# T5 attentions of a vision tower: scores per image on the rows of two heads, probabilities divided before they are turned, outputs made in turned form

## The chip, the cores and the metric

One core of a Trainium2 chip runs the whole tower in one launch. The metric is the device time in microseconds; shown are three runs of the kernel before and one profiled execution. TensorE's granted clock stands at one of two levels, 2.4 GHz (1.0 in the profile) or 1.2 GHz (0.5).

## The reference, cut to what matters

32 images of 37 tokens (a class token and 36 patches), width 192, 12 heads everywhere. The tower makes tokens, then three attentions with heads of 16 (neighbour, causal with a capacity MoE behind it, diagonal-masked), then four T5 layers, each an attention with heads of 64 and a feed-forward; the second and fourth of these have a routed MoE beside the dense one. Only the four T5 attentions compute something differently here:

```
q, k, v = nx @ attn_q[i], nx @ attn_k[i], nx @ attn_v[i]     # (b, 37, 12 heads, 64)
scores  = einsum('bqhd,bkhd->bhqk', q, k) + bias             # bias[h, q, k], the same for all images
attn    = softmax(scores, axis=-1)
ctx     = einsum('bhqk,bkhd->bqhd', attn, v).reshape(b, s, 768)
h       = h + ctx @ attn_o[i]
```

All in float32. There is no scale on the scores and no mask: each image attends to its own 37 tokens.

## The kernel before, in words

**Tiling.** Three images make a group of TG = 111 rows, 11 groups in all. Groups are taken in blocks of 3, 3, 3 and 2 for the q and k projections. A T5 attention has, per block, 12 QK steps (six chunks of q, then six of k; a chunk is 128 of the 768 columns, two heads, turned, so that tokens lie along the free axis), and per group two V steps (six heads each), two S steps, PT, PV, OT steps and a Y step.

**Order.** One list, PROGRAM, gives the order of the steps (`att_order`, line 351, and `att_fill`, line 297, for T5), and every engine walks the list and does its part of each step: there is no other scheduler, and each engine's queue is in order. The S steps of a layer are numbered n = 0 to 21 (group g = n // 2, half p = n % 2, six heads each). Between S(n) and S(n+1) stand, for the kernel before: slot 3p, the two PT of the half n-1 with slot 3p+1 between and behind them, E (exp) of the first three heads, PV of half n-2, slot 3p+2, E of the second three heads. The slots hold OT and Y of group g-2, the V of group g+1, the QK chunks of the next block (two in each of six slots, at the second and third group of a block), the turns "A" (of this layer's later groups and of the next stage's first), and, where a routed MoE follows, its logits L and counts CNT; W1 rounds and splits the next weights. A layer ends with PT, PV, OT and Y of the last groups, with no S beside them.

**What the steps do.** S on TensorE (line 1130): for each of three chunks, head 0 on rows 0-63 and head 1 on rows 64-127 by turns, a 111 x 111 score matrix of three images at once, into two PSUM banks (three heads in each). On DVE (`softmax_shift`, line 1587), for each bank: add the bias, which holds -1e30 where query and key are of different images (line 1593), negated maximum (1595), subtract it (1596). E on ACT: exp in place (1366). PT on TensorE (1033): three 111 x 111 transposes into the one bank ps_pt; ACT copies them out (1374). PV (1163): six heads, each with the turned probabilities as stationary operand and V with a column of ones (65 columns) moving, so the 65th output is the sum. DVE divides (`divide`, 1630: reciprocal 1640, product 1644) into `o`. OT (1180): three transposes of `o` into a projection bank, copied to `ot` by ACT (1352). Y (1191): six accumulated matmuls with `wo`; DVE adds to x (1781) and runs the norm's statistics (1552 to 1564). QK chunks are five matmuls in fp32r (1068), copied out by ACT in one instruction each (1319). An fp32 matmul that is no transpose leaves two records in the trace.

**Who waits.** A projection step needs its bank, one of two, back from the step two before it. S needs the bank of two scores ago back from DVE, PT the end of ACT's copy of the PT before, Y the copies of both OT.

Of the kernel before, what the change touches and what calls it, by code (L numbers as in the profile page):

```python
# [20 lines left out]
C = 192  # L21
# [37 lines left out]
class Att:  # L59
# [15 lines left out]

    def heads(self, u):

        return [(3 * (u // 2) + c, 64 * (u % 2)) for c in range(3)]

    def head(self, chunk, start):  # L80
        return 2 * chunk + start // 64
# [269 lines left out]
def att_order(a, last_stage, follower):  # L351
# [157 lines left out]
def numbered():  # L509
# [4 lines left out]
    for st, step in PROGRAM:  # L514
        key = (st, *step)
        if step[0] in ("TOK", "QK", "V", "OT", "Y", "U"):
# [3 lines left out]
        elif step[0] == "S":  # L520
            for e in range(2):
                score[(*key, e)] = len(score)
# [34 lines left out]
OUT_AT = {key: n for n, key in enumerate(OUTS)}  # L557
UNIT = {key: n for n, key in enumerate((_st[1], _step[1], _step[2]) for _st, _step in PROGRAM if _step[0] == "E")}
# [25 lines left out]
Y_BLOCK, Y_CAUSAL, Y_DIAG = [TG * i for i in range(3)]  # L584
Y_LNG, Y_LNB, Y_POS, Y_TOKB, Y_VB = [3 * TG + C * i for i in range(5)]
Y_WIDTH = 3 * TG + 5 * C
# [21 lines left out]
VWIDE = H * IPG * (SMALL_D + 1)  # L608
SHORT_V = 4 * 128
# [4 lines left out]
def tower(nc, patches, tok_w, consts, young, rows, gains, gates_w, head_scale, bias_src, wo_all, w1_all, w2_all, out, rows_in, rows_out):  # L614
    with ExitStack() as ctx:
# [22 lines left out]
        hscale = sb("hscale", [128, 4 * 2 * 3 + 4])  # L638
# [3 lines left out]
        relbias = sb("relbias", [TL, H, TG])  # L642
# [51 lines left out]
        v64 = sb("v64", [TG, 3, H, T5_D + 1])  # L694
# [6 lines left out]
        with ExitStack() as att_only:  # L701
            def sa(name, shape):
                return att_only.enter_context(nc.sbuf_tensor(name, shape, F32))
            qk = sa("qk", [128, 2, 12, 3 * TP])
            vimg = sa("vimg", [TG, 2, VWIDE])
            prob = sa("prob", [TG, 4, 3, TG])
            probt = sa("probt", [TG, 4, 3, TG])
            o = sa("o", [TG, 2, F])
# [48 lines left out]
        prob_ready = sem("prob_ready")  # L757
        pt_full = sem("pt_full")
        pt_taken = sem("pt_taken")
        o_full = sem("o_full")  # L760
        o_ready = sem("o_ready")
        gap_ready = sem("gap_ready")
# [20 lines left out]

        def short_q(slot):

            flat = qk[:, slot, 0:6, :].rearrange("p c n -> p (c n)")
            return flat[:, 0:2 * 3 * IPG * HWIDE].rearrange("p (j g i m) -> p j g i m", j=2, g=3, i=IPG)

        def short_k(slot):

            return qk[:, slot, 6:8, :]

        def neigh_kb(slot):

            return qk[:, slot, 8:10, :]

        def neigh_q(slot):

            return qk[:, slot, 10:12, :]

        scales = hscale[:, 0:24].rearrange("p (a j h) -> p a j h", a=4, j=2)
# [167 lines left out]
        def _(pe):  # L969
# [56 lines left out]
            def turn_prob(a, g, u):  # L1026
                n = unit(a, g, u)
                pe.wait_ge(prob_ready, n + 1)
                if n:
                    pe.wait_ge(pt_taken, n)  # L1030
                for i in range(4 if ATTS[a].short else 3):
                    src = short_ring(prob, n)[:, i * TG:(i + 1) * TG] if ATTS[a].short else prob[:, n % 4, i, :]
                    last = pe.transpose(ps_pt[0:TG, i * TG:(i + 1) * TG], src, ident)  # L1033
                last.then_inc(pt_full, 1)

            def att_step(st, step):
                a = st[1]
                s = ATTS[a]
                if step[0] in ("NX", "BD", "QS", "XA", "LATE", "W1", "LD", "ND"):
# [50 lines left out]
                elif kind == "S":  # L1090
                    p = step[2]
                    banks = [score_bank((*key, e)) for e in range(2)]
# [34 lines left out]
                    for i in range(3):  # L1127
                        for e, bank in enumerate(banks):
                            c, at = s.heads(2 * p + e)[i]
                            ins = pe.matmul(bank[0:TG, i * TG:(i + 1) * TG],  # L1130
                                            qk[at:at + 64, b % 2, c, t0:t0 + TG],
                                            qk[at:at + 64, b % 2, s.chunks + c, t0:t0 + TG],
                                            start=True, stop=True, skip_group_check=True)
                            if i == 2:
                                ins.then_inc(score_full, 1)
                elif kind == "PT":
                    turn_prob(a, g, step[2])
                elif kind == "PV":
                    p = step[2]
                    n = OUT_AT[(a, g, p)]  # L1140
                    pe.wait_ge(pt_taken, unit(a, g, 0 if s.short else 2 * p + 1) + 1)
                    pe.wait_ge(o_ready, OUT_AT[(a, g - 1, p)] + 1 if s.t5 and g else n)
# [15 lines left out]
                    for e in range(2):  # L1158
                        u = 2 * p + e
                        for i, (c, at) in enumerate(s.heads(u)):  # L1160
                            h = s.head(c, at)
                            col = (h % 6) * (s.d + 1)
# [3 lines left out]
                elif kind == "OT":  # L1166
                    bank = proj_bank(key)
                    j = step[2]
                    pe.wait_ge(o_ready, OUT_AT[(a, g, j if s.t5 else 1)] + 1)
                    if s.short:  # L1170
# [893 lines left out]
```

## Time and profile before

| | |
|---|---|
| median of 3 runs | 1876.59 us (1874.85 to 1884.35) |
| the profiled execution | 1864.46 us, span 1862.7 us |
| TensorE matmul / DVE / ACT / GpSimd busy | 86% / 57% / 43% / 27% of the span |
| mean granted clock | 0.86 |
| first S step of the four T5 layers | 588.9, 804.7, 1204.8, 1432.6 us |

The times are in microseconds from the span's start. Busy time of TensorE counts a matmul from its start to a modelled end, so that neighbours overlap; the distance from one start to the next is the better measure of what one costs. "PEld" is the loading of stationary operands, which runs beside the matmuls. In a timeline, "x12" merges twelve instructions of one line in a row, and a bracket names an idle time of the engine before them and what ended it.

### The profile page before, as it was taken

How to read it: one execution, taken by the hardware profiler on the slowest of the kernel's cores; microseconds unless marked ns; L12 is line 12 of the kernel's file. 1: busy time of each engine (PE TensorE's matmuls, PEld its weight loads, DVE VectorE, ACT ScalarE, POOL GpSimd, SP SyncE). 2: the span in 40 equal slices, each digit the busy share in tenths (PEclk: the TensorE clock that was granted, in tenths of full speed). 3: DMA queues.
4: the chain of work that ended last, by engine and by line, in shares of the span. 5: the costliest groups of instructions: out<-in, count | busy, mean ns of one | idle time of the engine just before them, and what ended most of it. 6: DMA issues, size and time to landing. Idle time of an engine off the chain costs nothing.

```text
span 1862.7 us, 33951 instructions
## 1 busy us (share of the span) xinstructions
PE 1595.3 (86%) x11921; PEld 1481.1 (80%) x11921; DVE 1068.1 (57%) x2975; ACT 810.0 (43%) x1971; POOL 511.8 (27%) x1259
## 2 busy tenths in 40 slices
PE   5898997895898998999977999788988999889980
PEld 4788776895777897888977999678878898779970
DVE  3675556333555776467775444377755778544437
ACT  1544431443555554355433555345534545255520
POOL 2245345005432112521322000453235123300031
PEclk6866765895567999999888999899999989899995
DMA  4120101451079000100004676300020000167731
GB/s 147 33 79 11 44 18 40 133 169 56 23 235 277 13 1 18 47 18 1 16 20 139 203 224 216 92 16 2 1 64 18 1 14 18 46 182 224 224 96 34
DMA packets 87756, 149.78 MB, mean 80 GB/s; under 512 B 7380, under 2 KB 58883, under 8 KB 87590
## 3 DMA queue, kind: packets, MB, share of 16 engines
q1 hardware_dynamic: 81254, 135.35, 23.7%
q0 software_dynamic: 6336, 12.26, 2.3%
q8 instruction: 98, 1.61, 0.4%
q14 instruction: 68, 0.56, 0.1%
HBM read 106.59 MB, written 41.05 MB: 79 GB/s over the span
## 4 chain that ended last, share of the span: by engine, by line
PE 54%; issue 22%; DVE 16%; ACT 3%; POOL 3%; DMA 2%; DVEq 0%; POOLq 0%; SPq 0%; ACTq 0%
PE ps_proj L1068 10%; PE ps_proj L1191 6%; PE ps_score L1262 5%; PE ps_proj L1082 5%; PE ps_proj L1245 4%; PE ps_o L1163 4%; PE ps_pt L1033 4%; PE ps_score L1119 4%; PE ps_o L1153 3%; PE ps_score L1130 2%; DVE prob L1596 2%; DVE prob L1593 2%; PE ps_proj L1049 2%; DVE negmax L1595 2%; PE ps_turn L1011 1%
## 5 line engine op out<-in xcount | busy, mean ns | idle before, releaser
L1262 PE MATMUL ps_score<-w,hid 128*112 128x192 f32 (+2 forms) x1680 | 303.0, 332 | 7.0 <-DVE x L1905 7.0
L1262 PEld LDWEIGHTS ps_score<-w,hid 128*112 128x112 f32 (+2 forms) x1680 | 275.3, 179 | 9.2 <-DVE x L1905 8.7
L1386 ACT ACTIVATE hid<-ps_proj 128x224 f32<-128x224 f32 (+2 forms) x360 | 137.5, 384 | 265.3 <-PE ps_proj L1245 265.2
L1493 POOL TENSOR_SCALAR tmp<-rs,var 111x1 f32<-111x1 f32 x110 | 40.5, 368 | 590.5 <-DVE rs L1564 590.0
L1451 POOL DMA_INDIRECT tin<-rows_out,idx x66 | 66.6, 1009 | 469.0 <-issue 365.4
L1033 PE MATMUL ps_pt<-const,prob 111*111 111x111 f32 x660 | 125.2, 307 | 36.8 <-ACT probt L1374 24.6
L1191 PE MATMUL ps_proj<-wo,ot 128*111 128x192 f32 (+1 forms) x616 | 136.3, 369 | 5.2 <-ACT ot L1352 5.0
L1033 PEld LDWEIGHTS ps_pt<-const,prob 111*111 111x111 f32 x660 | 93.5, 199 | 56.6 <-ACT prob L1366 24.1
L1374 ACT ACTIVATE probt<-ps_pt 111x333 f32<-111x333 f32 x176 | 78.7, 447 | 124.4 <-PE ps_pt L1033 123.8
L1163 PEld LDWEIGHTS ps_o<-v,probt 111*111 111x111 f32 x1056 | 124.6, 189 | 0.3
L1754 DVE TENSOR_TENSOR w_lo<-w_in,w_hi 128x768 fp32r<-128x768 f32 x65 | 62.3, 959 | 107.2 <-ACT w_hi L1410 106.3
L1191 PEld LDWEIGHTS ps_proj<-wo,ot 128*111 128x111 f32 (+1 forms) x616 | 110.1, 200 | 16.4 <-issue 13.9
L1163 PE MATMUL ps_o<-v,probt 111*111 111x65 f32 x1056 | 122.1, 269 | 0.0
L1366 ACT ACTIVATE prob<-prob 111x333 f32<-111x333 f32 (+1 forms) x209 | 102.4, 492 | 44.9 <-DVE prob L1596 42.7
L1319 ACT ACTIVATE qk<-ps_proj 128x336 f32<-128x336 f32 (+1 forms) x192 | 82.1, 428 | 78.6 <-PE ps_proj L1068 76.2
L1593 DVE TENSOR_TENSOR prob<-ps_score,relbias 111x333 f32<-111x333 f32 x176 | 88.9, 505 | 41.0 <-PE ps_score L1130 35.1
L1289 ACT ACTIVATE xa_hi<-ps_turn,gainf 128x111 fp32r<-128x111 f32 x132 | 46.3, 351 | 148.5 <-PE ps_turn L1011 130.5
L1245 PE MATMUL ps_proj<-ta_hi,w_hi 128*128 128x224 f32 (+1 forms) x264 | 94.6, 358 | 15.2 <-ACT hid L1386 11.3
L1068 PE MATMUL ps_proj<-xa_hi,w_hi 128*128 128x336 f32 (+2 forms) x244 | 91.8, 376 | 10.4 <-DVE xb L1734 9.6
L1596 DVE TENSOR_TENSOR prob<-prob,negmax 111x333 f32<-111x333 f32 x176 | 90.8, 516 | 6.1
L1595 DVE TENSOR_REDUCE negmax<-prob 111x3 f32<-111x333 f32 x176 | 88.0, 500 | 6.1
L1435 POOL DMA_INDIRECT rows_in<-xn,idx x66 | 64.4, 975 | 88.2 <-DVE idx L1851 34.4
(256 smaller groups left out, 4184.1 us busy)
## 6 DMA issues: line engine op xcount, KB each, us to landing
w_in<-w_all_dram SPq DMA_DIRECT2D x130, 384.0 KB, 3.3
w<-w_all_dram SPq DMA_DIRECT2D x50, 576.0 KB, 5.0
rows_in<-zero SPq DMA_DIRECT2D x1, 12320.0 KB, 46.8
rows_out<-zero SPq DMA_DIRECT2D x1, 9240.0 KB, 79.3
tin<-rows_in SPq DMA_DIRECT2D x36, 224.0 KB
rows_out<-tout SPq DMA_DIRECT2D x36, 168.0 KB
patch<-patches_dram SPq DMA_DIRECT2D x11, 333.0 KB, 2.9
wo<-wo_all_dram SPq DMA_DIRECT2D x6, 576.0 KB, 3.8
```

The source lines that it names most:

```text
L1033: last = pe.transpose(ps_pt[0:TG, i * TG:(i + 1) * TG], src, ident)
L1068: last = pe.matmul(bank[:, 0:n * TP], w[:, slot, c, at:at + 128], src, start=(i == 0), stop=(i == len(terms) - 1))
L1082: last = pe.matmul(bank[0:TG, 0:s.vwide], src[:, g, 0:TG], w[:, slot, c, at:at + s.vwide], start=(i == 0), stop=(i == len(terms) - 1 and a ...
L1163: last = pe.matmul(ps_o[0:TG, h // 6, col:col + s.d + 1], probt[:, unit(a, g, u) % 4, i, :], v64[:, g % 3, h, :], start=True, stop=True, s ...
L1191: last = pe.matmul(bank[0:TG, 0:C], ot[0:n, g % 2, c, :], w[0:n, c, :], start=(c == 0), stop=(c == len(parts) - 1))
L1245: last = pe.matmul(bank[:, 0:width], w[:, slot, c, m * 128:(m + 1) * 128], src, start=(n == 0), stop=(n == len(terms) - 1))
L1262: last = pe.matmul(bank[0:n, 0:C], hid[:, i % 2, m, at:at + n], w2[:, slot, m, :], start=(m == 0), stop=(m == FC - 1))
L1366: act.activation(p, p, ACT.Exp).then_inc(prob_ready, 1)
L1386: act.activation(hid[:, i % 2, m, 0:n], bank[:, 0:n], ACT.Relu if b.tile is None else ACT.Gelu).then_inc(taken, 1)
L1593: tell(dve.tensor_tensor(dst, scores, relbias[0:TG, 3 * u:3 * u + 3, :], ALU.add), taken, value)
L1595: link(dve.tensor_reduce(negmax[:, 0:3], scores, AX.X, ALU.max, negate=True))
L1596: ins = dve.tensor_tensor(dst, scores, negmax[:, 0:3].unsqueeze(2).to_broadcast([TG, 3, TG]), ALU.add)
```

## The change

It touches the four T5 attentions, and the layout of some tiles.

- **Scores.** The ACT copy of a q chunk is made twice, each with a scale of 1 on one head's 64 partitions and 0 on the other's, so that the chunk holds, per image, 37 columns of head 0 (rows of head 1 zero) and 37 of head 1 (`q_pairs`). S is nine matmuls (three chunks, three images) over all 128 rows, with the 74 q columns stationary and the image's 37 k columns moving. Scores lie on 74 rows (two heads), 3 chunks x 3 images x 37 columns, in one bank.
- **Softmax.** Add, maximum and subtract run once for the six heads; there is no mask in the bias. One exp. A new step DIV (`pair_divide`), at the end of the half, has DVE sum each row, take the reciprocal and multiply the probabilities; the semaphore `divided` releases the PT of the half.
- **PT.** One step a half: three transposes of 74 rows x 111 columns. ACT copies the result in three instructions, one an image, with a scale that is 1 on that image's key rows and 0 elsewhere.
- **PV.** V stationary (64 columns, no ones), turned probabilities moving (111 columns); heads 0 and 1 of a chunk go to PSUM partitions 0-63 and 64-127: the output comes out turned. `divide` is gone for T5; the OT step is an ACT copy alone, without TensorE, without a projection bank, and Y waits for it (`ot_ready`).
- The set-up's addition of the mask to the bias goes; the constants and the bias are smaller; `vimg` lies inside `qk`.

```diff
@@ att_order
-        for k in range(2):
-            if 1 <= n <= pairs:
-                h, q = divmod(n - 1, 2)
-                out.append(("PT", h, 2 * q + k))
-            out += slots[3 * p + k]
+        out += slots[3 * p]
+        if 1 <= n <= pairs:
+            out.append(("PT", *divmod(n - 1, 2)))
+        out += slots[3 * p + 1]
         if n < pairs:
-            out.append(("E", g, 2 * p))
+            out.append(("E", g, p))
         if n >= 2:
             out.append(("PV", *divmod(n - 2, 2)))
         out += slots[3 * p + 2]
         if n < pairs:
-            out.append(("E", g, 2 * p + 1))
+            out.append(("DIV", g, p))
@@ turn_prob (TensorE)
+                    pe.wait_ge(divided, n - unit(T5, 0, 0) + 1)
...
+                    for i in range(3):
+                        last = pe.transpose(ps_pt[0:TG, i * TWO:(i + 1) * TWO], prob[0:TWO, n % 4, i, :],
+                                            ident[0:TWO, 0:TWO])
@@ S (TensorE)
-                    for i in range(3):
-                        for e, bank in enumerate(banks):
-                            c, at = s.heads(2 * p + e)[i]
-                            ins = pe.matmul(bank[0:TG, i * TG:(i + 1) * TG],
-                                            qk[at:at + 64, b % 2, c, t0:t0 + TG],
-                                            qk[at:at + 64, b % 2, s.chunks + c, t0:t0 + TG],
+                    for c in range(3):
+                        for i in range(IPG):
+                            t, col = t0 + i * NTOK, (c * IPG + i) * NTOK
+                            last = pe.matmul(banks[0][0:TWO, col:col + NTOK],
+                                             q_t[:, 3 * p + c, (g - s.blocks[b][0]) * IPG + i, :, :]
+                                             .rearrange("p e q -> p (e q)"),
+                                             k_t[:, 3 * p + c, t:t + NTOK], start=True, stop=True,
...
@@ PV (TensorE)
-                            last = pe.matmul(ps_o[0:TG, h // 6, col:col + s.d + 1], probt[:, unit(a, g, u) % 4, i, :],
-                                             v64[:, g % 3, h, :], start=True, stop=True, skip_group_check=True)
+                            at = (2 * c + e) * TG
+                            last = pe.matmul(ps_o[64 * e:64 * e + 64, p, c * TG:(c + 1) * TG],
+                                             v64[:, g % 3, 2 * (3 * p + c) + e, :], turned_p[:, at:at + TG],
...
@@ QK and PT (ACT)
+                        for e in range(2):
+                            dst = q_pairs(b % 2)[:, j, 0:m * IPG, e, :].rearrange("p (g i) q -> p g i q", i=IPG)
+                            ins = act.activation(dst, src, ACT.Copy, scale=half[:, e:e + 1])
...
+                        for i in range(IPG):
+                            ins = act.activation(dst[:, :, i, :], src, ACT.Copy, scale=image[:, i:i + 1])
@@ DVE
+            def pair_divide(a, g, p):
+                dve.wait_ge(prob_ready, unit(a, g, p) + 1)
+                dst = pair_rows(a, g, p)
+                total = rden[0:TWO, 0:9].rearrange("p (c i) -> p c i", c=3)
+                link(dve.tensor_reduce(total, dst, AX.X, ALU.add))
+                link(dve.reciprocal(total, total))
+                tell(dve.tensor_tensor(dst, dst, total.unsqueeze(3).to_broadcast([TWO, 3, IPG, NTOK]), ALU.mult),
+                     divided, unit(a, g, p) - unit(T5, 0, 0) + 1)
```

## Rows read from the trace of the kernel before

**Rows 1.** The page's first part: busy us, share of the span, instructions.
```profile
PE 1595.3 (86%) x11921; PEld 1481.1 (80%) x11921; DVE 1068.1 (57%) x2975; ACT 810.0 (43%) x1971; POOL 511.8 (27%) x1259
```

**Rows 2.** Stretches: length, busy per engine (instructions), granted clock, DMA share, GB/s.
```profile
598.00:716.60 118.60, 114.21 (x955) 106.31 (x955) 84.37 (x208) 66.07 (x169) 19.48 (x56) 0.99 0.06 19
716.60:753.50 36.90, 27.94 (x207) 25.27 (x206) 23.59 (x62) 15.06 (x35) 11.38 (x32) 0.91 0.12 39
881.60:905.50 23.90, 21.99 (x144) 20.09 (x144) 17.07 (x61) 8.66 (x23) 6.74 (x12) 0.71 0.07 20
...
462.00:465.00 3.00, 3.00 (x31) 2.51 (x30) 2.65 (x9) 1.60 (x4) 0.00 (x0) 0.50 0.10 22
```

**Rows 3.** Timeline of TensorE, S(6,0) to S(7,0): start us, us, instruction, idle before.
```profile
670.80 0.84 PE L1130 MATMUL ps_score<-qk 64*111 64x111 f32 x12
...
675.10 0.36 PE L1011 MATMUL ps_turn<-const,xn 111*128 111x111 f32 x2
675.29 2.11 PE L1191 MATMUL ps_proj<-wo,ot 128*111 128x192 f32 x12
677.34 0.84 PE L1130 MATMUL ps_score<-qk 64*111 64x111 f32 x12
...
679.28 0.52 PE L1033 MATMUL ps_pt<-const,prob 111*111 111x111 f32 x3 [0.63 <-ACT probt L1374]
...
680.52 1.29 PE L1163 MATMUL ps_o<-v,probt 111*111 111x65 f32 x12
681.65 0.36 PE L1011 MATMUL ps_turn<-const,xn 111*128 111x111 f32 x2
...
682.23 0.84 PE L1130 MATMUL ps_score<-qk 64*111 64x111 f32 x12
```

**Rows 4.** Starts of S(1,0) and S(9,1), 17 halves apart, dense and routed layer.
```profile
600.68 0.64 PE L1130 MATMUL ps_score<-qk 64*111 64x111 f32 x3
...
716.63 0.35 PE L1130 MATMUL ps_score<-qk 64*111 64x111 f32 x2
...
811.91 0.35 PE L1130 MATMUL ps_score<-qk 64*111 64x111 f32 x2 [0.44 <-DVE prob L1593]
...
940.79 0.35 PE L1130 MATMUL ps_score<-qk 64*111 64x111 f32 x2
```

**Rows 5.** Timeline of DVE beside rows 3.
```profile
676.56 0.34 DVE L1734 SCALAR_TENSOR_TENSOR xb<-ps_turn,gainf,xb 64x111 fp32r<-64x111 f32 x1
677.50 0.36 DVE L1781 TENSOR_TENSOR x<-ps_proj,x 111x192 f32<-111x192 f32 x1 [0.60 <-PE ps_proj L1191]
...
679.14 0.50 DVE L1593 TENSOR_TENSOR prob<-ps_score,relbias 111x333 f32<-111x333 f32 x1
...
680.21 0.51 DVE L1596 TENSOR_TENSOR prob<-prob,negmax 111x333 f32<-111x333 f32 x1
...
682.39 0.20 DVE L1640 RECIPROCAL rden<-ps_o 111x6 f32<-111x6 f32 x1
```

**Rows 6.** Scaled copies of ACT (timeline), and two QK chunks in the chain.
```profile
545.17 1.40 ACT L1281 ACTIVATE qk<-ps_proj,hscale 128x333 f32<-128x333 f32 x3 [0.41 <-PE ps_proj L1068]
...
648.62 1.56 PE ps_proj L1068 x10
```

**Rows 7.** Timeline of TensorE: matmuls with 37 and 64 stationary columns.
```profile
78.97 1.29 PE L1153 MATMUL ps_o<-vimg,probt 111*37 111x51 f32 x24
...
462.46 0.64 PE L1007 MATMUL ps_turn<-const,x 111*64 111x111 f32 x4
462.98 0.39 PE L1153 MATMUL ps_o<-vimg,probt 111*37 111x51 f32 x2
```

**Rows 8.** The set-up's mask addition: duration ns, start, form.
```profile
L1672 DVE TENSOR_TENSOR relbias<-relbias,early x1: 1547/1547/1547, 95.1 to 95.1; 111x1332 f32<-111x1332 f32 x1
```

**Rows 9.** Timeline of TensorE: the last two Y of the dense layer.
```profile
738.39 3.47 PE L1191 MATMUL ps_proj<-wo,ot 128*111 128x192 f32 x12
...
745.63 2.17 PE L1191 MATMUL ps_proj<-wo,ot 128*111 128x192 f32 x12 [0.63 <-ACT ot L1352]
```

More of the change, by code:

```diff
@@ L515, in numbered @@
         key = (st, *step)
-        if step[0] in ("TOK", "QK", "V", "OT", "Y", "U"):
+        if step[0] in ("TOK", "QK", "V", "Y", "U") or step[0] == "OT" and ATTS[st[1]].short:
             proj[key] = len(proj)
@@ L520, in numbered @@
         elif step[0] == "S":
-            for e in range(2):
+            for e in range(2 if ATTS[st[1]].short else 1):
                 score[(*key, e)] = len(score)
@@ L1038, in att_step @@
                 s = ATTS[a]
-                if step[0] in ("NX", "BD", "QS", "XA", "LATE", "W1", "LD", "ND"):
+                if step[0] in ("NX", "BD", "QS", "XA", "LATE", "W1", "LD", "ND", "DIV"):
                     return
@@ L1091, in att_step @@
                     p = step[2]
-                    banks = [score_bank((*key, e)) for e in range(2)]
+                    banks = [score_bank((*key, e)) for e in range(2 if s.short else 1)]
                     b = s.block_of[g]
@@ L1165, in att_step @@
+                    for c in range(3):
+                        for e in range(2):
+                            at = (2 * c + e) * TG
+                            last = pe.matmul(ps_o[64 * e:64 * e + 64, p, c * TG:(c + 1) * TG],
+                                             v64[:, g % 3, 2 * (3 * p + c) + e, :], turned_p[:, at:at + TG],
+                                             start=True, stop=True, skip_group_check=True)
                     last.then_inc(o_full, 1)
-                elif kind == "OT":
+                elif kind == "OT" and s.short:
@@ L1181, in att_step @@
+                    for c, n in ((0, 128), (1, 64)):
+                        for i in range(IPG):
+                            at = c * TG + i * NTOK
+                            last = pe.transpose(bank[0:n, at:at + NTOK],
+                                                o[0:NTOK, g % 2, i * C + c * 128:i * C + c * 128 + n],
+                                                ident[0:NTOK, 0:NTOK])
                     last.then_inc(proj_full, 1)
@@ L1183, in att_step @@
                     bank = proj_bank(key)
-                    for j in range(s.vparts):
-                        proj_out((st, "OT", g, j))
+                    if s.short:
+                        proj_out((st, "OT", g, 0))
+                    else:
+                        pe.wait_ge(ot_ready, OUT_AT[(a, g, 1)] - OUT0 + 1)
                     if g == 0:
@@ L1759, in _ @@
                 elif kind == "S":
-                    if step[1:] == (0, 0) and st[1] == CAUSAL:
-                        link(dve.memset(v64[:, :, :, T5_D:T5_D + 1], 1.0))
                     if ATTS[st[1]].short:
@@ L1764, in _ @@
                     else:
-                        for e in range(2):
-                            softmax_shift(st, step[1], 2 * step[2] + e, (*key, e))
+                        softmax_shift(st[1], step[1], step[2], (*key, 0))
+                elif kind == "DIV":
+                    pair_divide(st[1], *step[1:])
                 elif kind == "PV":
-                    if (st[1], *step[1:]) in OUT_AT:
-                        divide(st[1], *step[1:])
+                    if ATTS[st[1]].short:
+                        divide(st[1], step[1])
                 elif kind == "Y":
```

185 lines of the change are left out of this document (84 added, 101 removed).

## The prediction

> **What bounds the kernel now.** I read the page first, then a table of stretches, then the order of time of each engine inside one T5 attention. TensorE is busy 86% of the span, DVE 57%, ACT 43% [rows 1]. In the body of the first T5 attention (598 to 716.6 us) TensorE is busy 114.2 of 118.6 us and DVE 84.4, so TensorE's own work sets the pace; in its tail (716.6 to 753.5) TensorE has 27.9 busy of 36.9, and DVE, which has fallen behind, sets it. The reader should also see that the second T5 stage has a stretch of 23.9 us at a granted clock of 0.71, a mix of the two levels, 2.4 and 1.2 GHz [rows 2]. I call a "half" what stands between two S steps (half a group: six heads of three images). A half with no QK projection and no Y takes 4.89 us, one with Y 6.54 [rows 3]. The 17 halves from group 1 to S(9,1) take 716.63 - 600.68 = 115.95 us in a dense-follower layer and 128.88 in a routed one [rows 4].
>
> **The change, part by part, TensorE first.** Scores: six matmuls (12 records) become nine (18). 12 PV records with 111 weight columns take 1.13 us, 0.094 each; records with 37 weight columns take 1.29/24 = 0.054 [rows 3, 7]. With 74 weight columns and 37 moving I take 0.063, near 74/111 of the first: 18 x 0.063 = 1.14 us, between 0.97 and 1.69. Turning probabilities: one step of three instead of two, about 0.3 us (one is 0.29 now: PT and V together are 1.24 from 679.28 to 680.52), and the wait of the second for ACT's copy of the first (0.63) goes [rows 3]. PV: 12 records with 64 weight and 111 moving columns, written by turns to PSUM partitions 0-63 and 64-127. The only such pair takes 0.52 us for four records at half clock, so 0.065 each at full [rows 2, 7]: 12 x 0.06 = 0.72 us instead of 1.13. Bounds: 0.05, and about 0.10 if the two column halves did not overlap (111 moving columns against 0.054 for 51). The turning of the outputs (OT) leaves TensorE, some 0.35 us a half. Together TensorE's work falls by about 0.85 us a half.
>
> The Trainium skill ("TensorEngine Tiling (Array Packing)", Performance Considerations) says that stationary free dimensions of at most 64 give up to twice the rate by column tiling. No row here shows fp32 PV in that form at full clock; by that rule PV would be 0.6 us a half, the serial price 1.2.
>
> DVE: two times (add, max, subtract) a half become one, 1.6 us less (two such steps take 1.07 [rows 5]); reciprocal and product of the outputs (about 0.8) become sum 0.53, reciprocal 0.20, product 0.53 on the probabilities. Net about 1.1 us less a half. ACT: one exp less; three scaled copies of 333 elements take 1.40 together, 0.43 apart and 0.54 the last [rows 6]. The two copies of the turned probabilities (333 elements each) become three with a scale (222 each), about 1.1 instead of 0.8. Each q chunk is copied twice: 0.97, of which 0.87 hold ACT, where TensorE makes a chunk in 0.78 (two in 1.56 [rows 6]). The mask add of 1.55 us goes [rows 8]; smaller loads: nothing, they are under other work.
>
> **The new wait.** DIV(n) stands on DVE behind everything in the half's last slot: A, Y, L, CNT, W1. The next half's PT on TensorE waits for it, and behind PT in TensorE's order stand QK, V, PV and Y. Before, PT waited for exp alone, and DVE's shift stood ahead of Y. From rows: after a Y, the next S starts at 677.34, Y's add at 677.50, the norm is done by 679.14, 1.80 after S started [rows 3, 5]. Then sum 0.53, reciprocal 0.20, product 0.53, 0.14 to TensorE: PT can start 3.2 us after S started. S takes 1.14, so TensorE idles 2.1 us. After an A: turn at 675.10, DVE's second part done at 676.90, S would start 0.2 after the turn: 1.6 + 1.4 = 3.0, an idle time of 1.9 [rows 3, 5]. With projections between S and PT (1.55 us for two chunks) 0.3 to 0.5 stay.
>
> **Adding up.** Halves of a dense layer, 17 of them. After Y, no projections (2): 3.2 + 1.24 (PT, V) + 0.72 + 0.2 (A) = 5.36 against 4.89, +0.5 each. After A, no projections (5): 3.0 + 1.24 + 0.72 + 2.24 (A and Y) = 7.2 against 6.54, +0.65 each. One with neither: unchanged. With projections (9): 0.85 less work, but about 0.4 of DIV wait (3.0 or 3.2 against S and two chunks, 2.7) and about 0.45 of waits for ACT's q copies: 0. For these, take the half with four q chunks: chunks end at 1.9 and 2.7 us, PT at 3.4; ACT copies q0 until 3.0, q1 until 3.8, the probabilities until 4.9, q2 until 5.7; V needs q2's bank, so it starts at 5.7 where TensorE would be free at 4.9: 0.8. In the next half the probabilities' copies push the sixth chunk's followers back by 0.3. Sum +4.2 us a dense layer. In a routed layer L (1.3 of DVE) and CNT (1.0) also stand before DIV, but before has the 0.71 clock stretch there: +2.8. Four layers: +14. First block of projections: six q copies over TensorE by 0.09 each, +2 in all.
>
> Tail, dense: S(9,1) to the end of the last Y takes 31.0 us now (716.63 to 745.63 and the Y's 2.0 [rows 4, 9]). New: DIV(9,0) done at 3.1, shift 4.7, weight split until 8.3, DIV(9,1) 9.6, PT, PV, A, Y(8) 13.0, its norm 14.8, DIV(10,0) 16.1, shift and exp 18.3, DIV(10,1) 19.7, then PT, PV, Y, PV, copy, Y: 26.4. That is -4.6 at full clock, and by the same laying out -5.9 in a routed layer: -21. But now a Y takes 3.47 us at half clock in the tail where it is 2.05 at full [rows 3, 9], with PV and turns about 3.1 us for the tail; the new tail idles as long (3.4 us in front of PT(9,1)), and since I left its half clock out of the 26.4, 4 x 3.1 = +12.4. In the body I take one further fall of the clock a layer: a stretch of many 8-column matmuls was followed by 1.2 GHz (23.9 us at 0.71 [rows 2]), and the new halves idle 2 us in 5 to 7. One half at half clock costs its PT, V, PV, A and with Y: 2.2 to 4.4 us, I take 3: +12.
>
> Sum: 14 + 2 - 21 + 12.4 + 12 - 1.5 = +18 us. The profiled execution took 1864.5 us (span 1862.7), so 1882.5 by it; the median of the runs is 1876.6, 12 above, so I forecast **1894**. 0.5%, some 9 us, is what a measurement of this kernel tells from no change.
>
> **Rivals.** (a) The work counts, not the wait: DVE is 2.2 us a group lighter and ACT's PT wait goes, so TensorE would stay full. 76 halves x 0.85 = 65 and the tail's 21 less: 1877 - 86 = about 1790; with half of it 1835. For: 96% busy body [rows 2]. Against: DIV's place behind Y. It decides if DIV comes within 1.2 us of S, which rows 5 speak against. (b) Slower: idle 2 us in every half without projections lets the clock fall there: 9 halves x 3 us x 4 = +108, about 1990. It needs falls at most waits; against it, the present tail is busy only 27.9 of 36.9 us and its mean clock is still 0.91 [rows 2]. (c) The column halves do not overlap: PV 1.2 instead of 0.72, 80 x 0.5 = +40 on the forecast, 1934.
>
> **Chances.** Forecast 0.50, (a) whole or in half 0.27, (b) 0.13, (c) 0.10. Own terms of the forecast: PV at 0.05 -10, no q wait -13, no fall in the body -12, tail at full clock -12; scores at 0.094 in the halves with projections +20, two more falls +24. That gives 1847 to 1938; I give 1842 to 1940. Faster by over 0.5%: 0.27 and 0.06 of the forecast, 0.33; within 0.5%: 0.19; slower: 0.25 + 0.23 = 0.48.
>
> **What would show it.** In the new profile TensorE should wait for DVE's product in front of PT, some 2 us after a Y or A and under 0.5 with projections between; 0.063 us a score record, 0.06 a PV record; halves of 5.4 and 7.2 us; V waiting for q copies; DVE busy in T5 down by a quarter. Wrong if the waits in front of PT are short, if halves fall to 4.1 and 5.9 us, or if the clock in the T5 bodies falls well below 0.95.

## The result, and the profile after

The changed kernel takes **1952.7 us** (median of 4 runs, 1945.5 to 1965.2) where the kernel before took 1875.8 beside it: ratio 1.041, 95% interval 1.037 to 1.045. The forecast was 1894 with a range of 1842 to 1940: the sign was right, the size was not, and the range did not hold it. The profiled execution has a span of 1946.4 us (before 1862.7) at a mean granted clock of 0.83 (before 0.86).

The page's first part, of the changed kernel, against [rows 1]: DVE has lost 97 us of work, TensorE's busy time has not fallen.

```profile
PE 1614.0 (83%) x11921; PEld 1469.7 (76%) x11921; DVE 970.7 (50%) x2797; ACT 830.2 (43%) x2067; POOL 519.5 (27%) x1259
```

The four stretches from S(0,0) to S(9,1), first of the kernel before, then of the changed one. Columns as in [rows 2].

```profile
588.89:716.63 127.74, 118.60 (x992) 109.91 (x991) 92.17 (x227) 71.20 (x182) 22.20 (x67) 0.97 0.12 38
804.74:940.79 136.05, 127.88 (x1040) 119.53 (x1039) 100.66 (x279) 69.42 (x176) 27.00 (x64) 0.95 0.03 8
1204.83:1343.96 139.13, 122.71 (x992) 112.38 (x991) 105.82 (x276) 70.82 (x177) 50.91 (x128) 0.96 0.02 6
1432.55:1568.70 136.15, 127.95 (x1040) 119.52 (x1039) 100.57 (x279) 69.42 (x176) 26.97 (x64) 0.95 0.03 8
```

```profile
586.00:728.38 142.38, 120.94 (x1002) 106.17 (x1002) 72.11 (x190) 73.74 (x198) 24.14 (x67) 0.92 0.09 29
818.91:978.15 159.24, 133.09 (x1052) 117.14 (x1051) 80.26 (x242) 72.12 (x193) 29.28 (x64) 0.85 0.02 7
1243.43:1397.61 154.18, 126.78 (x1003) 111.43 (x1002) 85.86 (x239) 73.27 (x194) 51.98 (x128) 0.87 0.02 6
1489.98:1650.53 160.55, 134.85 (x1052) 119.28 (x1051) 80.33 (x242) 72.02 (x193) 28.75 (x64) 0.84 0.02 7
```

These 616.4 us were 539.1 before: 77.3 of the 83.7 us that the span grew stand here. A stretch of granted clock c stood 2(1 - c) of its length at half clock. That makes 46 us before and 162 after. Where TensorE works through it, time at half clock is twice what it would be at full, so the 116 us more of it are worth up to 58. At least 19 are waits and work. Behind S(9,1) the layers, with the feed-forwards and the end, grew by 9.3, and all that lies ahead of the first T5 layer shrank by 2.9.

How it comes about is seen in one half, S(3,1) to S(4,0), which has no projection chunk of q or k (TensorE, then DVE, then stretches around it):

```profile
633.83 1.33 PE L1146 MATMUL ps_score<-qk 128*74 128x37 f32 x18
637.06 0.65 PE L1047 MATMUL ps_pt<-const,prob 74*111 74x74 f32 x3 [1.90 <-DVE prob L1640]
637.45 0.64 PE L1097 MATMUL ps_proj<-w_hi,xa_hi 128*111 128x384 f32 x1
...
639.30 1.38 PE L1182 MATMUL ps_o<-probt,v 111*64 111x111 f32 x12
640.61 0.44 PE L1018 MATMUL ps_turn<-const,xn 111*128 111x111 f32 x2
640.89 1.33 PE L1146 MATMUL ps_score<-qk 128*74 128x37 f32 x18
```

```profile
634.09 0.36 DVE L1796 TENSOR_TENSOR x<-ps_proj,x 111x192 f32<-111x192 f32 x1 [0.60 <-PE ps_proj L1207]
...
635.72 0.50 DVE L1638 TENSOR_REDUCE rden<-prob 74x9 f32<-74x333 f32 x1
636.25 0.21 DVE L1639 RECIPROCAL rden<-rden 74x9 f32<-74x9 f32 x1
636.50 0.50 DVE L1640 TENSOR_TENSOR prob<-prob,rden 74x333 f32<-74x333 f32 x1
```

```profile
627.88:633.83 5.95, 5.66 (x54) 5.12 (x53) 3.38 (x8) 3.35 (x10) 0.00 (x0) 1.00 0.02 4
633.83:637.06 3.23, 1.33 (x21) 1.22 (x18) 2.66 (x10) 0.00 (x0) 1.06 (x3) 1.00 0.00 0
637.06:640.61 3.55, 3.55 (x21) 2.76 (x21) 1.48 (x3) 1.98 (x5) 2.04 (x6) 0.53 0.00 0
640.61:643.86 3.25, 1.61 (x22) 1.49 (x20) 1.90 (x6) 1.27 (x4) 0.00 (x0) 0.98 0.00 0
643.86:647.39 3.53, 3.53 (x21) 2.75 (x21) 1.48 (x3) 1.98 (x5) 0.00 (x0) 0.54 0.00 0
```

The norm behind Y ends, DIV's three instructions follow, and PT starts 3.23 us after S, as foretold (3.2). But the clock is 0.53 in the stretch right behind the 1.90 us of idle time, is back at 0.98 while TensorE waits once more, and falls again behind the next wait. It is low where there is work and high where there is none. In the 17 halves from S(1,0) on, six waits of the first T5 layer in front of PT were 1.64 to 1.90 us long. The clock fell behind four of them (halves of 7.06, 8.75, 8.78 and 8.60 us) and stayed up behind two: one of 1.64 us at 724.12, and one of 1.90 us, as long as the one above, in a half of 5.56 us:

```profile
686.40 0.51 PE L1047 MATMUL ps_pt<-const,prob 74*111 74x74 f32 x3 [1.90 <-DVE prob L1640]
```

```profile
686.40:688.73 2.33, 2.33 (x22) 1.91 (x23) 1.48 (x3) 1.78 (x5) 1.89 (x6) 1.00 0.00 0
```

S(1,0), with 7.55 us, had its low clock (0.50) already from a wait of 3.17 us in the half before. In the bodies of all four layers, 16 waits of 1.5 to 2.0 us in front of PT ended at full clock; behind 11 of them the clock fell within 2 us. So the length of one wait alone does not decide whether the clock falls, and what else does was not tested.

The kernel's whole wait in front of PT (TensorE's waits: us, times, longest):

```profile
PE ps_pt L1047 <- DVE prob L1640: 119.0, 75, 5.2
```

### The profile page after: what moved, and what is told of

It reads as the page before. It is cut to its first block, busy times and chain, and to the rows that moved or that the text cites. A ratio compares the mean times of both kernels' runs of the same rounds, so it can differ in the third digit from the quotient of the medians.

```text
span 1946.4 us, 33513 instructions
## 1 busy us (share of the span) xinstructions
PE 1614.0 (83%) x11921; PEld 1469.7 (76%) x11921; DVE 970.7 (50%) x2797; ACT 830.2 (43%) x2067; POOL 519.5 (27%) x1259
## 3 DMA queue, kind: packets, MB, share of 16 engines
q1 hardware_dynamic: 81254, 134.81, 22.3%
## 4 chain that ended last, share of the span: by engine, by line
PE 49%; issue 22%; DVE 17%; ACT 9%; POOL 2%; DMA 1%; SPq 0%; DVEq 0%; POOLq 0%; ACTq 0%
PE ps_proj L1207 7%; PE ps_proj L1097 7%; PE ps_proj L1083 7%; PE ps_score L1278 5%; PE ps_o L1182 4%; PE ps_proj L1261 4%; PE ps_score L1134 4%; PE ps_o L1172 3%; ACT qk L1342 3%; PE ps_pt L1047 2%; DVE prob L1640 2%; DVE rden L1638 2%; PE ps_turn L1018 2%; ACT probt L1406 2%; PE ps_proj L1064 1%
## 5 line engine op out<-in xcount | busy, mean ns | idle before, releaser
L1406 ACT ACTIVATE probt<-ps_pt,const 111x222 f32<-111x222 f32 x264 | 99.0, 452 | 220.9 <-PE ps_pt L1047 220.7
L1747 DVE SCALAR_TENSOR_TENSOR xa_lo<-ps_turn,gainf,xa_hi 128x111 fp32r<-128x111 f32 x132 | 43.9, 333 | 239.6 <-ACT xb L1306 238.0
L1047 PE MATMUL ps_pt<-const,prob 74*111 74x74 f32 x264 | 54.6, 326 | 119.0 <-DVE prob L1640 119.0
L1047 PEld LDWEIGHTS ps_pt<-const,prob 74*111 74x111 f32 x264 | 41.2, 217 | 131.7 <-DVE prob L1640 131.7
L1146 PEld LDWEIGHTS ps_score<-qk 128*74 128x74 f32 x1584 | 129.8, 161 | 4.4 <-issue 2.8
L1146 PE MATMUL ps_score<-qk 128*74 128x37 f32 x1584 | 131.9, 246 | 1.4 <-ACT qk L1335 1.4
L1342 ACT ACTIVATE qk<-ps_proj,hscale 128x333 f32<-128x333 f32 (+1 forms) x192 | 84.2, 529 | 63.1 <-PE ps_proj L1083 63.1
L1182 PE MATMUL ps_o<-probt,v 111*64 111x111 f32 x1056 | 92.2, 325 | 0.0
L1018 PE MATMUL ps_turn<-const,xn 111*128 111x111 f32 x242 | 58.0, 330 | 41.1 <-POOL xn L1545 15.7
L1182 PEld LDWEIGHTS ps_o<-probt,v 111*64 111x64 f32 x1056 | 68.6, 174 | 27.8 <-issue 14.3
```

Source lines behind the costliest of these rows:

```text
L1018: last = pe.transpose(ps_turn[:, c * TP:c * TP + TG], xn[0:TG, g, c * 128:(c + 1) * 128], ident)
L1047: last = pe.transpose(ps_pt[0:TG, i * TWO:(i + 1) * TWO], prob[0:TWO, n % 4, i, :], ident[0:TWO, 0:TWO])
L1146: last = pe.matmul(banks[0][0:TWO, col:col + NTOK], q_t[:, 3 * p + c, (g - s.blocks[b][0]) * IPG + i, :, :] .rearrange("p e q -> p (e q)") ...
L1182: last = pe.matmul(ps_o[64 * e:64 * e + 64, p, c * TG:(c + 1) * TG], v64[:, g % 3, 2 * (3 * p + c) + e, :], turned_p[:, at:at + TG], start ...
L1342: ins = act.activation(dst, src, ACT.Copy, scale=half[:, e:e + 1])
L1406: ins = act.activation(dst[:, :, i, :], src, ACT.Copy, scale=image[:, i:i + 1])
```

## The experiments

Two halves are followed through them: S(3,1), behind a Y, and S(4,0), behind an A, with a Y of its own. Lengths in us, from one S start to the next:

| | before | forecast | after | e3 | e2 | e7 | e9 |
|---|---|---|---|---|---|---|---|
| S(3,1) | 4.88 | 5.36 | 7.06 | 5.55 | 3.47 | 9.51 | 6.67 |
| S(4,0) | 6.56 | 7.2 | 8.75 | 7.25 | 6.23 | 9.56 | 7.92 |

**e1, e2: is it the place of DIV?** e1 puts DIV one slot ahead of Y, A and the weights; e2 also exp one slot ahead.

```diff
+        out += slots[3 * p + 1]      (e1; in e2 behind E)
         if n >= 2:
             out.append(("PV", *divmod(n - 2, 2)))
-        out += slots[3 * p + 2]
         if n < pairs:
             out.append(("DIV", g, p))
+        out += slots[3 * p + 2]
```

> The step DIV stands ahead of the half's last slot (before A, Y, L, CNT and W1) instead of behind it; nothing else is changed. Theory D (the new wait in front of PT, with the falls of the clock that follow it, makes the loss): PT could start 1.9 us after the S of a half without projections instead of 3.0 to 3.2, so the wait is 0.7 or less, such halves take 4.0 to 4.6 us (6.0 to 6.5 with Y) instead of 7.06 and 8.75, the clock in the T5 bodies stays near 1.0, the 17 halves of the dense layer's body take 107 to 115 us instead of 132.8, and the whole 1850 to 1880 us instead of 1953. Theory W (the loss is the pace of ACT's copies, and short score matmuls that hold the clock low whatever the waits): 1925 to 1955 us, clock as in the changed kernel, waits in front of PT replaced by others.

> As e1, and exp (E) also stands ahead of slot 3p+1, so that on ACT it is not behind the V copy or the q copies of that slot. Theory D: the last 0.7 us of wait in front of PT in halves without projections goes (they are few): 5 to 15 us less than e1, 1840 to 1870 us. Theory W: exp waits for DVE's shift with q copies behind it on ACT, so TensorE waits for banks in halves with projections: 5 to 20 us more than e1.

Measured: e1 1843.0 us, faster than expected (1850 to 1880), ratio to the kernel before 0.981 (0.977 to 0.986); e2 1838.8, 0.981 (0.978 to 0.985), and once more beside e10 1838.9, 0.980 (0.976 to 0.984). The place of one DVE step decides between 4% slower and 2% faster; exp adds nothing that these runs can tell. In e2 the two halves together run at full clock, and the waits are a third:

```profile
625.61:635.31 9.70, 9.06 (x93) 8.10 (x92) 7.79 (x22) 5.58 (x16) 2.85 (x8) 1.00 0.01 2
```

```profile
PE ps_pt L1047 <- DVE prob L1640: 38.7, 21, 5.5
```

**e3: how much of it is the clock?** The wait stays where it is, but TensorE does useless work in it: 14 bf16 matmuls into an unused part of ps_pt's bank, in the halves without QK between S and PT. The wait for ACT's copy of the PT before, whose bank the filling writes, stands ahead of it.

```diff
+                    if (a, g, u) in FILL:
+                        for _ in range(14):
+                            pe.matmul(ps_pt[0:TG, 300:512], identb[:], mask[:, 0:212], ...)
                     pe.wait_ge(divided, n - unit(T5, 0, 0) + 1)
```

> The changed kernel with 14 bf16 matmuls of 212 columns (results unused) on TensorE in front of each T5 PT that has no projections between it and S, where TensorE idles about 2 us. They take 1.3 us at 2.4 GHz, inside the wait. Theory D with the clock as its larger part: the clock no longer falls at these waits, PT, V and PV go back to full rate, the dense body takes 120 us instead of 132.8 (my forecast's 120.2 held no falls), in all 35 to 55 us less than 1953: about 1905. Rival (the chain through DVE sets the time, the clock is beside it): within 10 us of 1953, or up to 15 more where the filling outlasts the wait.

Measured: 1896.7 us, ratio 1.011 (1.007 to 1.015), 56 below the changed kernel, though TensorE has more to do. S(3,1) and the stretch of the two halves (e3's line numbers are 13 higher):

```profile
621.64 1.33 PE L1159 MATMUL ps_score<-qk 128*74 128x37 f32 x18
622.80 1.47 PE L1050 MATMUL ps_pt<-maskb,identb 111*111 111x212 bf16 x14
624.87 0.51 PE L1060 MATMUL ps_pt<-const,prob 74*111 74x74 f32 x3 [0.59 <-DVE prob L1653]
```

```profile
621.64:634.44 12.80, 11.86 (x123) 10.59 (x121) 8.20 (x22) 5.58 (x16) 3.10 (x8) 1.00 0.01 1
```

PT still starts 3.23 us after S. The first body takes 127.7 us (132.8 without the filling), not the 120 expected: the halves with projections stay long, and where the wait was short, as in S(3,0) with 0.29 us, the filling itself costs 0.8. The halves take 5.55 and 7.25 where the forecast had 5.36 and 7.2: in these halves the piece by piece sum was right at full clock, and what it missed are the falls. The profiled execution is 50.8 us shorter: 30 of them in the four stretches, 11 behind them, and 10 ahead of the T5 layers, where the two kernels do the same and which is chance. So the falls are worth at least 41 us, since the filling itself takes time, and by the clock up to 58 in the stretches alone.

**e4: do the copies of q set the pace of the halves with projections?** One more scaled copy of each T5 q chunk on ACT, which overwrites the tower's saved rows, so that its output is not the reference's.

```diff
+                        spare = held[...][:, j * 333:j * 333 + m * TG]...
+                        act.activation(spare, src[0:TG], ACT.Copy, scale=half[0:TG, 0:1])
```

> The changed kernel with one more scaled ACT copy of each T5 q chunk, into memory that nothing reads: 0.43 us more of ACT a chunk, 24 chunks a layer, 10 us a layer. If the q copies already set the pace where they stand (my 0.45 us a half with projections), nearly all of it shows: +25 to +40 us over 1953. If ACT has slack there, under +8 us.

Measured: 1980.9 us (ratio 1.056, 1.050 to 1.062), +28 on the changed kernel for 96 copies: 0.29 us each, of 0.43 that one holds ACT. So ACT is on the path there, but for how much of a copy stays open: the halves with projections stood some 30 us longer at half clock than in the changed kernel, which is worth up to 15 of the 28. This run shows the point on single waits once more: S(3,1), again with 1.90 us in front of PT, takes 5.55 us here at a clock of 1.00.

**e5, e8: can that be had back?** e5 makes the chunks as q, k, q, k in e2; e8 gives the q copies to DVE, in e5.

```diff
+def qk_order(s):
+    return [6 * e + j for j in range(6) for e in range(2)] if s.t5 else list(range(s.qk))
...
+                elif kind == "QK" and st[1] >= T5 and step[2] < 6:       (e8, DVE)
+                    for e in range(2):
+                        ins = dve.tensor_scalar(dst, src, half[:, e:e + 1], None, ALU.mult)
```

> The kernel of e2_exp_ahead (exp and DIV ahead of the work of the later slots), and in the T5 layers the QK chunks are made as q, k, q, k instead of six q and then six k: a q chunk needs two ACT copies, a k chunk one, so ACT is no longer behind for three q chunks in a row. Theory (ACT's copies of the q chunks hold up V and QK in the halves with projections): nine halves a layer lose about 0.45 us each, 4 x 9 x 0.45 = 16 us less than e2's 1839, about 1823 (1815 to 1830); the waits of V and QK for qk <- ps_proj (3.5 + 3.5 us in the first body of e2) fall under 2 us. Rival (those waits are covered by other work): 1835 to 1843, no change.

> The kernel of e5_q_k_by_turns, with both scaled copies of each q chunk made by DVE (two multiplications from PSUM) instead of ACT; ACT keeps the k chunks. e5 lost nothing by turns of q and k, so not the order of the copies but their sum on ACT may bound the halves with projections. Theory (ACT's sum bounds them): the nine halves with projections, 75.7 us in the first body of e2, fall toward the 68.9 of the kernel before less 0.85 each, about 61 to 65: 4 x 11 = 45 us less, 1795 to 1815, with no V or QK waiting for qk. Rival 1 (they are bound by TensorE and by the clock at the first halves): 1835 to 1845. Rival 2 (DVE's copies, about 0.85 us a chunk in front of DIV, bring the wait in front of PT back): 1850 or more, with ps_pt <- prob above 80 us.

Measured: e5 1845.7 us (0.984, 0.980 to 0.987), no gain; e8 1913.7 (1.021, 1.017 to 1.025). The theory behind e8 fell: DVE takes its steps in order, so the q copies stand behind the softmax of the new scores, and TensorE waits for their bank. The timeline of e8 inside S(4,1), DVE and TensorE, and its waits for these copies:

```profile
654.16 1.03 DVE L1789 TENSOR_SCALAR qk<-ps_proj,hscale 128x333 f32<-128x333 f32 x2
655.25 0.42 PE L1088 MATMUL ps_proj<-xa_hi,w_hi 128*128 128x336 f32 x1 [1.82 <-DVE qk L1789]
```

```profile
PE ps_proj L1088 <- DVE qk L1789: 52.7, 40, 2.7
```

Rival 2 had the size (1850 or more) but not the place: PT's wait stayed at 37.7 us. A half with QK that took 8.3 us in e2 takes 9.3 at full clock. Besides, e8's halves with projections stood 72 us at half clock, e5's 14, so up to 29 of the 68 us between the two runs are falls of the clock.

**e6: do the two column halves of PV overlap?** In e2, the three matmuls for PSUM partitions 0-63 first, then the three for 64-127.

```diff
-                    for c in range(3):
-                        for e in range(2):
+                    for e in range(2):
+                        for c in range(3):
```

> The kernel of e2_exp_ahead with the six PV matmuls of a half in another order: the three that write PSUM partitions 0-63 first, then the three for 64-127, instead of by turns. If the two column halves of TensorE overlap only between neighbours, PV goes from 0.72 to about 1.2 us for 12 records: 84 halves x 0.4 = +35 us, about 1870. Rival (no overlap of the columns at all: 0.06 us a record is simply what 111 moving columns behind 64 weight columns cost): PV stays at 0.72 and the time at 1839, within 8 us.

Measured: 1854.8 us, ratio 0.989 (0.985 to 0.992); e2 with 0.981 lies some 15 us lower. PV takes 0.97 us from its start to the turn behind it, where e2 has 0.72, as has the changed kernel (there 630.91 to 631.63):

```profile
628.33 1.03 PE L1182 MATMUL ps_o<-probt,v 111*64 111x111 f32 x12
629.30 0.41 PE L1018 MATMUL ps_turn<-const,xn 111*128 111x111 f32 x2
```

So 0.060 us a record by turns and 0.081 in a row: 0.25 us x 88 = 22 us, of which some 15 show. The order alone makes this difference, as it would if the two column halves overlapped between neighbours; how it comes about in TensorE, and whether three in a row overlap at all, these runs do not show. The serial price of 1.2 us is met in neither order, and the expected 0.4 a half was too much.

**e7, e9: the wait alone, on the kernel before.** e7 adds to the kernel before nothing but a sum and a reciprocal on DVE at DIV's place, and the wait of the next half's first PT for it. e9 is e7 with 18 filling bf16 matmuls in front of the wait.

```diff
+            out.append(("DIV", g, p))                       (at the end of a half)
...
+                if ATTS[a].t5 and u % 2 == 0:
+                    pe.wait_ge(divided, (n - unit(T5, 0, 0)) // 2 + 1)
...
+                link(dve.tensor_reduce(rden[:, 24:27], prob[:, n % 4, :, :], AX.X, ALU.add))
+                tell(dve.reciprocal(rden[:, 27:30], rden[:, 24:27]), divided, ...)
```

> The kernel before, with the new wait alone: at the end of each half DVE sums three heads' probabilities and takes a reciprocal (about 0.55 + 0.2 us; the numbers are not used), and the first PT of the next half waits for that. Scores, softmax, division and PV stay as they were. PT can then start about 2.7 us after S behind a Y or an A, where S takes 1.10: TensorE idles 1.4 to 1.6 us in 7 halves a layer without projections, about 0.2 in those with them. Theory (the wait itself, by DIV's place behind Y, and falls of the clock that it sets off): 4 x (7 x 1.5 + 10 x 0.2) = +50 us for the waits and, if the clock falls as in the changed kernel, +40 more: 1925 to 1970. Rival 1 (the wait without falls of the clock; these come from the many short score matmuls): about 1928 with no more time at half clock than before. Rival 2 (the wait costs nothing without the other edits): within 10 us of 1877.

> The kernel of e7_wait_alone with 18 bf16 matmuls of 179 columns into an unused part of the bank of ps_pt in front of the wait, in the halves without QK between S and PT, as e3 did for the changed kernel. e7 took 2090, 212 above the kernel before. Theory (most of the 212 are falls of the clock, not idle time): the waits stay as idle or filled time, 7 x 1.8 us in a body of 17 halves and some in the tail, 4 x (12.6 + 5) = 70 us, so about 1950 (1930 to 1975), and the halves without projections take 6.6 and 8.3 us at full clock (1.8 above the kernel before). Rival (DVE's added work and the later chain make the 212 themselves): above 2040.

Measured: e7 2090.0 us, ratio 1.112 (1.106 to 1.117); e9 1992.2, 1.062 (1.057 to 1.066). Both are above what was expected. e7's TensorE, a wait at full clock, five chunk matmuls of 0.32 at full clock, and then the fall (0.48); its 17 halves from S(1,0); and those of e9:

```profile
660.56 0.84 PE L1134 MATMUL ps_score<-qk 64*111 64x111 f32 x12
663.17 0.52 PE L1037 MATMUL ps_pt<-const,prob 111*111 111x111 f32 x3 [1.77 <-issue]
...
664.47 0.32 PE L1072 MATMUL ps_proj<-xa_lo,w_hi 128*128 128x336 f32 x1
664.62 0.42 PE L1072 MATMUL ps_proj<-xa_hi,w_lo 128*128 128x336 f32 x1
664.84 0.48 PE L1072 MATMUL ps_proj<-xb,w_hi 128*128 128x336 f32 x1
```

```profile
595.97:754.78 158.81, 133.10 (x946) 123.90 (x945) 95.32 (x240) 66.14 (x168) 20.28 (x56) 0.85 0.04 11
```

```profile
605.06:747.04 141.98, 136.58 (x1253) 127.56 (x1252) 95.28 (x240) 65.42 (x168) 20.23 (x56) 1.00 0.04 13
```

The same 17 halves took 115.95 us before [rows 4]. Filled, they take 26 more at a clock of 1.00; idle, another 17 at 0.85. Over the kernel the wait, with DVE's added work and the filling, is worth about 117 us (e9) and the falls about 94 (0.050 between the two ratios). The wait alone, with the old scores, brings the falls, so the many short score matmuls are not needed for them. The size was missed because the wait is met in more places (64, 114.8 us in all) than the 28 that were counted. The text on the order of the kernel before puts the work of slot 3p ahead of PT, but there it stands behind the first PT: `att_order` has PT and then the slot, and the `att_order` part of the change's diff moves the slot ahead. In S(4,1) of the kernel before PT follows S directly, and the chunks come behind it; in the changed kernel two chunks (650.80 to 652.43) stand between S and PT:

```profile
647.31 0.84 PE L1130 MATMUL ps_score<-qk 64*111 64x111 f32 x12
648.08 0.54 PE L1033 MATMUL ps_pt<-const,prob 111*111 111x111 f32 x3
648.39 0.40 PE L1068 MATMUL ps_proj<-xa_hi,w_hi 128*128 128x336 f32 x1
```

```profile
652.86 0.51 PE L1047 MATMUL ps_pt<-const,prob 74*111 74x74 f32 x3 [0.27 <-DVE prob L1640]
```

So nothing covers e7's wait in the halves with projections: the nine of its first body wait 13.5 us in front of PT, those of the changed kernel 2.7. The move is part of what makes the wait cheaper in the changed kernel, and e7 is a harder test than the wait of the changed kernel alone. The wait costs the old kernel 212 us and the new one 114 (changed kernel less e2). The 33 halves with projections of the four layers have 76 of these 98 us: they grew by 74 from the kernel before to e7, and take 298 us in e2 and 296 in the changed kernel.

**e10, e12: a better place for A.** In e2 the turns A of the next block, one slot earlier, in front of PV and DIV: all three (e10), or the last alone (e12).

```diff
-            places = ... if late else [(0, 2), (0, 5), (1, 2)]
+            places = ... if late else [(0, 1), (0, 4), (1, 1)]     (e10)
+            places = ... if late else [(0, 2), (0, 5), (1, 1)]     (e12)
```

> The kernel of e2_exp_ahead with the turns A of the next block one slot earlier (in front of PV and DIV instead of behind them), so that QK(1,0) right behind S(1,1) has its turned rows. In e5's first T5 body this QK waited 1.43 us for xb and the clock fell right behind it (0.93 and 0.73 in the two stretches of 5 us from 595); e2 has 12.0 us of such waits in ten places. Theory: the waits of ps_proj <- xb in the T5 layers go (4 x 1.4 us) and with them the fall of the clock there (4 x about 2.5 us): 14 to 18 us less than e2, about 1823. Rival 1 (the first halves fall to half clock anyway, from the 1.9 us wait in front of PT(0,0)): 1833 to 1840. Rival 2 (DVE's split now stands in front of DIV and makes PT wait longer): above 1840.

> The kernel of e2_exp_ahead with only the last of the three turns of a block one slot earlier, the one behind which QK comes in the next half. In e10 all three stood ahead of DIV: where no projection stands between S and PT, PT then waited 2.37 us (636.10 to 639.86) instead of 0.63 and the clock fell, so that half took 9.58 us instead of 6.23. Theory: that loss goes, since QK covers the later DIV here, and the gain of e10 in S(1,1), 8.2 instead of 10.4 us, stays: 4 x 2 us less than e2, about 1831 (1822 to 1836). Rival (S(1,1) is slow for another reason, the half clock that the first waits set off): 1836 to 1842, as e2.

> The kernel of e2_exp_ahead once more, beside e10 on one chip, for the size of e10's difference: 1832 to 1845, ratio 0.978 to 0.984 to the kernel before.

Measured: e10 1862.5 us (0.992, 0.989 to 0.995), e12 1848.0 (0.982, 0.978 to 0.986), e2 beside e10 0.980. Rival 2 of e10 held: the split of A now delays DIV. S(4,0) in e10, then in e2's second run:

```profile
636.10 1.39 PE L1146 MATMUL ps_score<-qk 128*74 128x37 f32 x18
639.86 0.61 PE L1047 MATMUL ps_pt<-const,prob 74*111 74x74 f32 x3 [2.37 <-DVE prob L1640]
...
642.37 1.34 PE L1182 MATMUL ps_o<-probt,v 111*64 111x111 f32 x12
```

```profile
631.63 1.33 PE L1146 MATMUL ps_score<-qk 128*74 128x37 f32 x18
633.59 0.51 PE L1047 MATMUL ps_pt<-const,prob 74*111 74x74 f32 x3 [0.63 <-DVE prob L1640]
...
634.94 0.79 PE L1182 MATMUL ps_o<-probt,v 111*64 111x111 f32 x12
```

The half takes 9.58 us instead of 6.23: 1.74 more of waiting, and the rest by the fall behind it (PV 1.34 instead of 0.79). It happens twice in the first body (3.35 and 3.05 us), where S(1,1) gives 2.2 back; the four stretches together are 22.8 us longer than in e2's second run, and 24 were measured in all. e12 was no better than e2: S(1,1), which starts at 592.9, still takes 10.5 us, and its clock is 0.50 up to 598.4, as its rival had it. Also S(4,0) takes 8.29 us in e12, at a clock of 0.79: PT waits 0.63 us there as in e2, where the clock stayed up, and A another 0.32. e2 is the best version found, 2% under the kernel before.

## Why the prediction was wrong

**The step that failed** is "In the body I take one further fall of the clock a layer", with 3 us for it and +12 in the sum. 116 us more at half clock in the four stretches say up to +58, and filling the waits gives at least 41 back in the T5 layers (e3). Rival (b) had this mechanism, "idle 2 us in every half without projections lets the clock fall there", at +108 and a chance of 0.13; it falls in most of them, not in all, and costs about half of that. The evidence put against it was poor: that the old tail "is busy only 27.9 of 36.9 us and its mean clock is still 0.91" is a mean over 37 us, and that tail had already a Y at 3.47 us [rows 9]. The Trainium skill ("TensorE: Matmul & The Clock Gate", HAM oscillation) describes just this, a wait in each turn of a loop that costs each turn its clock, but the rule that it states there is for idle gaps longer than the 1.6 to 2.4 us behind which the clock fell here; the measurement decides.

**The wait itself** was about right in dense layers: 2 x 2.1 + 5 x 1.9 + 9 x 0.4 = 17.3 us by the forecast's terms, and 14.4 us of idle time in front of PT in the 17 halves of the first body (11.6 in the eight without projections, 2.7 in the nine with them). The forecast counted from start to start, by which a wait is some 0.17 us longer than its idle time (3.23 less 1.16 is 2.07, where the row has 1.90). In a routed layer it was priced below a dense one (+2.8 against +4.2), because the old kernel has its slow stretch there. But where L and CNT stand ahead of DIV it is longer, and the slow stretch stayed. The second stretch of the changed kernel waits 22.3 us; S(9,0) there, 7.59 us before, takes 11.81, and its PT:

```profile
966.34 1.37 PE L1146 MATMUL ps_score<-qk 128*74 128x37 f32 x18
970.85 0.83 PE L1047 MATMUL ps_pt<-const,prob 74*111 74x74 f32 x3 [3.14 <-DVE prob L1640]
```

So the dense stretches grew by 14.6 and 15.1 us, the routed by 23.2 and 24.4.

**The tail**: -21 + 12.4 = -9 forecast; what follows S(9,1) grew by 9.3 instead. The first tail takes 31.8 us (728.38 to 760.2) against 31.0. Four PT waits of 1.90, 1.39, 1.89 and 2.27 us stand in it, and its clock is 0.73 (before, from 716.6 to 747.6, 0.89), which is worth up to 8.6 us, where the forecast had 3.1. Whether the 26.4 us laid out at full clock were right no run shows: e2's tail takes 26.9 us, but with DIV ahead of the weight split and at a clock of 0.81. The changed kernel's tail, then e2's:

```profile
728.38:760.20 31.82, 23.73 (x172) 20.80 (x170) 16.21 (x43) 10.26 (x26) 7.38 (x21) 0.73 0.08 26
```

```profile
704.49:731.35 26.86, 21.23 (x172) 18.79 (x169) 15.41 (x42) 10.35 (x26) 7.08 (x21) 0.81 0.10 31
```

**The halves with projections**: 0 forecast; the nine of the first body take 73.3 us after and 68.9 before, +0.5 each. The waits were as laid out in the half from 649.64: PT 0.27, V 0.64 for a q copy, in the next 0.30. But each costs more than its idle time: the chunks' matmuls start 0.15 apart, and PT starts 0.58 behind the last of them, so 0.27 of idle time cost 0.43, and V's 0.64 cost 0.82. And the "0.85 less work" was too much. From start to start, against the same half before, S takes 0.39 more (1.16, before 0.77 from 647.31), PT 0.23 less, PV 0.41 less and OT 0.37 less: 0.62. That makes +0.63 of the 0.85 us by which this half grew; the rest is open. e5 says that the order of ACT's q copies does not matter; that their sum holds these halves is argued from e4 and not shown.

**What was right**: DIV behind Y and A is late, and the work saved in a half does not pay for it. PT starts 3.23 us after S (3.2). 18 score records take 1.16 us (649.64 to 650.80; 1.14), PV 0.72 (0.72), and halves at full clock are as long as forecast (e3: 5.55 and 7.25). DVE is lighter by a fifth in the first stretch, 92.2 to 72.1 us. Rival (a) fell as told, by DIV's place; without that wait the kernel takes 1839 to 1843 (e1, e2), near its half (1835) and not its whole (1790). Rival (c) fell: PV takes 0.72 us a half and not 1.2.

**In sum**, of the profiled executions, +83.7 us (by the medians +77) where +18 was forecast: -2.9 ahead of the T5 layers; +77.3 in the four stretches, with 28 forecast (14, 2 and 12 for the clock); +9.3 behind them, with -9 forecast. Of the 77.3, the 35 halves without projections from S(1,0) on have 57.4, where 26 were forecast; they stood 105 us longer at half clock, which is worth up to 52. The 33 halves with projections have 19.3, where 0 was forecast, and the first two halves of the layers 0.6. (The forecast took nine halves with projections in every layer; the third has six.)

## What to carry to other kernels

When a new wait of about 2 us is put in front of TensorE in every turn of a loop, price it twice: the idle time, and everything that runs behind it at half clock until the clock is back. Here the second was half or more of the loss. One wait may leave the clock up and the next of the same length not, so a chance belongs in the price. Put the producer ahead of all that its engine does for later steps before anything else is tuned: two lines of order turned +4% into -2%. And look for falls of the clock in single rows (a known instruction at twice its length), never in a mean over tens of us.

## What the runs showed of the hardware

- Idle times of 1.64 and 1.90 us (changed kernel), 1.77 us (e7) and 2.37 us (e10) of TensorE were followed by 1.2 GHz within 1.5 us. Others of 1.64 and 1.90 us (changed kernel, at 724.12 and 686.40) were not: of 16 such waits in the changed kernel's T5 bodies, 11 were. With waits of 0.63 us the clock stayed at 1.00 in e2; in the same half of e12 it fell behind waits of 0.63 and 0.32 us. Useless bf16 matmuls in the wait kept 2.4 GHz, and were worth 56 us (e3) and some 94 (e9 against e7).
- fp32 matmuls with 64 stationary and 111 moving columns that go to the two column halves by turns take 0.060 us a record, in a row 0.081.
- fp32 matmuls with 74 stationary and 37 moving columns take 0.064 us a record (1.16 for 18).
- A scaled copy of 128 x 333 from PSUM takes 0.43 us a piece on ACT in a row, and 1.03 for two on DVE.
